# One-hots of the sort in 16 bits by sixteen instructions, their product on VectorE, and ctx splits behind the first gathers

## The reference

```python
x = x + xattn(layernorm(x), itok, ctx, ctx, ctx)     # Wg = Wu = Wd = ctx
x = x + ffn(layernorm(x), G, gate_w, up_w, down_w, lora_A, lora_B)

# xattn
tid = clip(token_ids, 0, 24999); expert_ids = minimum(tid // 6250, 3)
for e in range(4):
    y = (silu(h @ Wg[e].T) * (h @ Wu[e].T)) @ Wd[e].T
    out = where(expert_ids == e, y, out)

# ffn: scores = softmax(x @ G), top 2 of 8, w = their values in a row of 8
out = sum_e w[e] * ((silu(x @ gate_w[e].T) * (x @ up_w[e].T)) @ down_w[e].T + (x @ lora_A[e].T) @ lora_B[e].T)
```

## Time and profile before

| what | before |
|---|---|
| median of 3 runs | 313.19 us (311.81 to 313.78) |
| the profiled execution | 313.26 us |
| its span, first to last instruction | 311.5 us |
| PE busy | 266.6 us (86%) |
| DVE busy | 236.1 us (76%) |
| POOL busy | 168.6 us (54%) |
| ACT busy | 149.6 us (48%) |
| mean granted clock of TensorE | 0.925 |

### The profile page before, as it was taken

One profiled execution on the slowest core, in us unless ns is written; L12 is line 12 of the kernel. 1 busy time (PEld: TensorE's weight loads), 2 busy tenths in 40 slices (PEclk: granted clock), 3 DMA queues, 4 the chain that ended last, 5 costly groups with the idle time before them and its releaser, 6 DMA issues. The chain is left out here.

```text
span 311.5 us, 6118 instructions
## 1 busy us (share of the span) xinstructions
PE 266.6 (86%) x1629; PEld 230.0 (74%) x1629; DVE 236.1 (76%) x726; ACT 149.6 (48%) x350; POOL 168.6 (54%) x173
## 2 busy tenths in 40 slices
PE   0568999999999999999599949859999999999910
PEld 0546787888888887888488839748999899999700
DVE  8686848779987998799838985888999986666600
ACT  4532433444444445435324433226666678888810
POOL 3659425443488638863672181427544427867760
PEclk9958999999999999999789995679999999999965
DMA  7562999611043114410333035259977756999830
GB/s 272 198 207 76 337 241 333 233 34 38 0 157 103 36 34 170 162 43 2 136 137 102 2 136 170 80 149 313 303 245 208 216 176 92 208 247 151 106 51 0
DMA packets 23280, 45.98 MB, mean 148 GB/s; under 512 B 4540, under 2 KB 8636, under 8 KB 22656
## 3 DMA queue, kind: packets, MB, share of 16 engines
q0 software_dynamic: 9488, 21.84, 25.9%
q1 hardware_dynamic: 13760, 23.74, 25.2%
HBM read 24.49 MB, written 25.80 MB: 161 GB/s over the span
## 5 line engine op out<-in xcount | busy, mean ns | idle before, releaser
L399 POOL DMA_INDIRECT out<-pair_out,dest_now x38 | 49.8, 1311 | 32.5 <-DVE pair_out L924 13.4
L475 ACT ACTIVATE aT_hi<-p_aT 128x512 fp32r<-128x512 f32 x19 | 11.4, 600 | 55.3 <-PE p_aT L1038 55.3
L1112 PE MATMUL p_y<-ctx_hi,aT_hi 128*128 x76 | 32.6, 429 | 0.3 <-ACT aT_hi L475 0.3
L1112 PE MATMUL p_h<-ctx_hi,xT_hi 128*128 x72 | 29.9, 416 | 1.4 <-ACT xT_hi L471 1.4
L350 POOL DMA_INDIRECT xin<-x,gather_row x19 | 20.3, 1070 | 19.7 <-DVE rec L725 15.6
L1113 PE MATMUL p_y<-ctx_lo,aT_hi 128*128 x76 | 30.9, 406 | 0.0
L372 POOL DMA_INDIRECT rows_a<-rec,dest x19 | 18.9, 996 | 21.8 <-DVE dest L799 17.1
L1113 PE MATMUL p_h<-ctx_lo,xT_hi 128*128 x72 | 28.4, 395 | 0.0
L357 POOL TENSOR_TENSOR rstd<-var_eps,neg_half 128x1 f32<-128x1 f32 x19 | 12.7, 670 | 26.8 <-DVE var_eps L694 24.0
L1058 PEld LDWEIGHTS p_rt<-route_w,x2T 128*128 128x128 f32 x152 | 20.5, 198 | 3.9 <-issue 2.5
L486 ACT ACTIVATE rec<-rec,neg_mean 128x512 f32<-128x512 f32 x19 | 13.7, 723 | 18.3 <-DVE var_eps L734 17.4
(11 more groups left out here) (254 smaller groups left out, 792.7 us busy)
## 6 DMA issues: line engine op xcount, KB each, us to landing
whole<-ctx_t SPq DMA_DIRECT2D x4, 1024.0 KB, 6.7
pair_x_late<-rows_b SPq DMA_DIRECT2D x14, 258.0 KB, 4.3
pair_x_early<-rows_a SPq DMA_DIRECT2D x12, 258.0 KB, 3.2
pair_x_late<-rows_a SPq DMA_DIRECT2D x10, 258.0 KB, 3.7
whole<-w_up SPq DMA_DIRECT2D x4, 576.0 KB, 6.3
rows_a<-pair_x_early SPq DMA_DIRECT2D x8, 258.0 KB, 11.8
rows_b<-pair_x_early SPq DMA_DIRECT2D x8, 258.0 KB, 12.6
pair_x_early<-rows_b SPq DMA_DIRECT2D x8, 258.0 KB, 3.2
```

Of the source, the lines that this page charges most:

```text
L399: nc.gpsimd.indirect_dma_start(out=out, out_offset=bass.IndirectOffsetOnAxis(ap=rows, axis=0), in_=pair_out[:, s % ORING, :], in_offset=No ...
L1112: nc.tensor.matmul(to, hi(i), w_hi(i), start=(i == 0), stop=False)
```

## The change

Five edits.

- `col_h` is a 16 bit copy of `col` (0 to 127 in each partition), kept in the first columns of `x2T`, which isn't in use yet. `slot_lo` becomes a 32 bit float tensor copied from `slot_low`.
- The one-hots are sixteen tensor_scalar instructions of 128 numbers, with 16 bits in and out, and `slot_lo[:, c]` as a scalar for each partition. A semaphore is raised after every fourth, and TensorE waits for each group of four.
- The product `put[:, :, 0, :]` is made by DVE, ahead of the one-hots, and no longer by POOL.
- DVE's first split waits for `gathers_asked`, which a small POOL memset raises behind gathers 0 and 1. The DVE order becomes split (0,0), statistics(0), statistics(1) with normalise(0) inside, split (1,0), lo_x(0), normalise(1), split (1,1), split (2,0), statistics(2), split (2,1).
- `WARM` is 52 for 40.

```diff
-WARM = 40
+WARM = 52
+        col_h = x2T[:, 0:P // 2].bitcast(F16)
-        slot, slot_lo, slot_hi = (scrap(1980 + TILES * i, TILES).bitcast(I32) for i in range(3))
+        slot, slot_low, slot_hi = (scrap(1980 + TILES * i, TILES).bitcast(I32) for i in range(3))
+        slot_lo = scrap(2130, TILES)
+        gathers_asked = sem("gathers_asked")
...
-            pool.wait_ge(owners_ready, 1)
-            nc.gpsimd.tensor_tensor(put[:, :, 0, :], put[:, :, 1, :],
-                                    token_f.unsqueeze(2).broadcast_to([P, TILES, STEPS]),
-                                    ALU.mult).then_inc(puts_ready, 1)
             pool.wait_ge(rows_ready, 2)
             gather(0)
             gather(1)
+            nc.gpsimd.memset(x2T[:, D - 1:D], 0.0).then_inc(gathers_asked, 1)
             split_ctx(0, 1, ctx_lo_half_ready)
...
+            nc.vector.tensor_copy(col_h, col[:])
...
-            nc.vector.tensor_scalar(slot_lo, slot, P - 1, None, ALU.bitwise_and)
+            step(nc.vector.tensor_scalar(slot_low, slot, P - 1, None, ALU.bitwise_and))
+            nc.vector.tensor_copy(slot_lo, slot_low)
             step(nc.vector.tensor_scalar(slot_hi, slot, P.bit_length() - 1, None, ALU.logical_shift_right))
...
-            for half in range(2):
-                shape = [P, TILES // 2, P]
-                some = slice(half * TILES // 2, (half + 1) * TILES // 2)
-                nc.vector.tensor_tensor(in_lo[:, some, :], col[:].unsqueeze(1).broadcast_to(shape),
-                                        slot_lo[:, some].unsqueeze(2).broadcast_to(shape),
-                                        ALU.is_equal).then_inc(onehots_ready, 1)
+            dve.wait_ge(owners_ready, 1)
+            nc.vector.tensor_tensor(put[:, :, 0, :], put[:, :, 1, :], token_f.unsqueeze(2).broadcast_to(to_steps),
+                                    ALU.mult).then_inc(puts_ready, 1)
+            for c in range(TILES):
+                last = nc.vector.tensor_scalar(in_lo[:, c, :], col_h, slot_lo[:, c:c + 1], None, ALU.is_equal)
+                if c % 4 == 3:
+                    last.then_inc(onehots_ready, 1)
...
+            dve.wait_ge(gathers_asked, 1)
             split_ctx(0, 0)
-            split_ctx(1, 0)
             statistics(0)
             statistics(1, between=0)
-            split_ctx(1, 1)
+            split_ctx(1, 0)
             lo_x(0)
             normalise(1)
+            split_ctx(1, 1)
             split_ctx(2, 0)
...
-                if c % (TILES // 2) == 0:
-                    pe.wait_ge(onehots_ready, c // (TILES // 2) + 1)
+                if c % 4 == 0:
+                    pe.wait_ge(onehots_ready, c // 4 + 1)
```

## The result

The changed kernel takes 315.26 us in the median of 18 runs (314.38 to 316.7) against 313.06 for the kernel before in the same rounds (310.76 to 314.92): ratio 1.0077, 95% interval 1.0054 to 1.01, so it is 1.7 to 3.1 us slower. Forecast were 315.2 us and a difference of +2.0. The profiled execution took 315.98 us (span 314.2, before 311.5), somewhat over the median.

The account below looks back on a forecast made before the run. TensorE was taken to set the pace from 27.2 to 100 us, but at 34.16 to wait for the chain from statistics(2). That starts +1.4 and +0.6, so +2.0 us, later: 315.2 us on 313.19, range 312.3 to 317.0.

Parts of the forecast that it names:

- Where it decides: At 34.16 us, step 1's transposes of act wait for the DVE, POOL, DVE chain from statistics(2), without slack.
- Ahead of the one-hots: In the sort: waiting step, copy, shift and product on DVE start the first one-hot at 7.00 instead of 6.29, +0.71.
- The one-hots: In the sort: sixteen at 0.17 us each, 2.7 us in all; L658 starts +0.6 us later (-0.3 to +2.1).
- The first gather: With DVE idle until both gathers issue, it takes 1.0 us instead of 2.18; both done at 13.13, against 13.67.
- Rival 3: The first gather's 2.18 us is its own, not DVE's: +1.2 more, 316.4 us; chance 0.14.
- issues at 10.85, takes 1.0: The first gather issues at 10.85 instead of 10.21 and takes 1.0 us instead of 2.18.
- Who gets the port: Both first splits released at 13.13; POOL's goes first, DVE's stands until 15.55; normalise(0) at 18.45, +1.4 us.
- The order behind: Three splits between normalise(0) and statistics(2) instead of two: +1.13 less 0.51 idle, +0.6; statistics(2) at 24.2, +2.0.
- The sum: +2.0 us at step 1's transposes (36.2 for 34.16) carried to the end: 315.2 us on the median of 313.19.
- I see nothing later that gives it back: Behind the chain at 34.16 TensorE is full, so the +2.0 us stays to the end.
- rival 5: The lateness is taken up by a later load, or splits lie otherwise: within 0.5 us of before, 313; chance 0.08.
- The warm matmuls: Ahead of step 0: twelve more end near 14.7 us while TensorE is idle to 19.0, and cost nothing.

Follow-up runs that it names:

- run 1: The sort alone: one-hots, product and 52 warm matmuls as changed, splits as in the kernel before, no wait for gathers; 313.6 us, ratio 1.0033.
- run 2: The order alone: the kernel before with the new wait for gathers, the new split order and 52 warm matmuls; 314.06 us, ratio 1.0077.
- run 3: The changed kernel, but POOL's first split waits for DVE's split (0,0); 315.24 us, ratio 1.0064.
- run 5: The changed kernel plus one 128x1 POOL product when half the one-hots are made, before the first gather; 315.72 us, ratio 1.0088.
- run 4: The changed kernel with three sets of sixteen extra DVE instructions ahead of the one-hots, to price them; its one execution took 326.66 us.
- run 6: The changed kernel with 40 warm matmuls for 52; 315.46 us, ratio 1.0084.
- run 7: The kernel before with its start rebuilt (three gathers first, splits and constants moved), 40 or 84 warm matmuls; 313.1 and 313.03 us, ratios 1.0018 and 1.0014.
- run 8: The rebuilt start on the kernel before, constants moved to step 3, with 40, 84 or 104 warm matmuls; ratios 0.9976, 0.9974, 0.9994.

## Why the prediction was right, point by point

- **Where it decides.** Right: the chain from statistics(2) through POOL's splits to the transposes of step 1 carried the delay without slack (+2.88 at both ends; +0.32 and +0.31 in run 1, +1.03 and +1.01 in run 2, +1.59 and +1.57 in run 3, +2.27 and +2.24 in run 5).
- **Ahead of the one-hots.** +0.71 forecast, +0.98 measured (6.29 to 7.27). The term I left out is the copy of `col_h`: begun at 1.63 us it takes 0.81, while POOL's memsets run to 2.35, and the sort behind it comes 0.26 us later. The one-hots give 0.19 us back where 0.09 were forecast, so L658 of before starts 0.79 us late for +0.6.
- **The one-hots.** 0.17 us each forecast, 0.163 measured, and the terms behind it as well (run 4). Named once more, the rule of the Trainium skill (VectorE: DVE Perf Modes, the section on the TRN2 errata), 0.094 us: it comes near the immediate's 0.109 and leaves out the pointer's 0.054.
- **The first gather.** Rival 3 fell: alone it takes 1.16 us (run 2). The inference in the Trainium skill (SBUF — State Buffer, "Practical consequences"), that a two-input instruction doesn't hold up descriptor generation, does not fit: DVE's subtraction held this gather's issue for 1.0 us. The runs don't tell whether the writing of descriptors or the reading of `gather_row` out of SBUF was held. What failed is the step "issues at 10.85, takes 1.0": it issued at 11.65. 0.65 us of that is POOL's late start after a long idle time, which I hadn't priced; I had written the removal of POOL's product down as worth nothing, and it cost 0.65 (run 5). Another 0.15 is the sort (+0.79 at gather_row for +0.64) and 0.16 the gather itself (1.16 for 1.0). Gathers done at 14.10 for 13.13 forecast.
- **Who gets the port.** Right in kind and size: POOL first, the split at 3.36 us for "about 3.4"; run 3 takes just this away and normalise(0) comes 0.84 us earlier; the 1.31 us at step 1 hold some 0.4 of the clock.
- **The order behind.** +0.6 forecast from normalise(0) to statistics(2), +0.54 measured (25.08 - 19.37 against 22.20 - 17.03). Run 2, where it was +0.14 (23.23 - 17.92), shows that this term hangs on the clock: with the transposes at the upper clock DVE has no wait for lo_x(0).
- **The sum.** +2.0 forecast at step 1, +2.88 measured: 0.9 us too little, from 0.65 + 0.15 + 0.16 above. "I see nothing later that gives it back" was wrong by as much: 0.86 us is given back at step 3, as rival 5 had it in part. That the two cancel is luck, and so is the rest of the way in the trace, where the clock gives 0.9 and takes 1.4. The time, +2.2 us, so agrees better than its parts. What the times themselves bear out is that the order alone costs as much as the whole change by the ratio (1.0077 both) and the sort alone about 1 us; that the order costs it through the block stands on the traces.
- **The warm matmuls.** Nothing, as forecast (run 6).

Open: why the order alone is 1.3 us (medians) to 2.4 us (ratio) slower in time while its trace lags by 0.2 to 1.0; why neither the block taken away (run 3) nor the earlier gather (run 5) shows in the time; and whether the stretches at the lower clock, worth 0.9 and 1.4 us in these traces, follow from the kernel or change from one execution to the next.

## What to carry to other kernels

When a semaphore frees VectorE at the moment when GpSimd goes on to a long operation of two inputs in SBUF, expect that one of the two stands for the whole of the other's operation, and what is queued behind it too. The one that began 0.08 us earlier went first, POOL's split here and DVE's split against the first gather of the kernel before; but in the earlier trace rows POOL went first though its record begins 0.06 us later. A wait that fixes the order (run 3) is surer than a small difference in start. An operation taken off an engine can have been worth more than its result, and a cast "for later" that stands ahead of a serial chain is a term of the sum. A gain or loss of 2 us at a kernel's start is worth following to its end: a transfer whose landing did not move with the start took back 0.9 here.

## What the runs showed of the hardware

- GpSimd, idle for 9.3 us (changed kernel) or 16.5 (run 4), began an indirect DMA 0.95 us after its last input was written; having worked up to 2 us before, 0.30 (before, runs 2 and 5).
- An indirect DMA's issue of 1.16 us took 2.18 beside a two-input subtraction on VectorE that had begun 0.08 us earlier (before and run 2).
- Sixteen tensor_scalar of 128 numbers on VectorE: 0.109 us each with an immediate, 0.163 with a pointer scalar (16 bits), 0.204 from 32 bit integers.
- A small operation was held as the large ones were: 0.17 us became 4.36 behind two GpSimd subtractions in a row, and it wasn't let in between them (run 7).
- TensorE's clock stayed at its upper level for 2.3 us after the warm matmuls of the kernel before (13.0 to 15.3), and for some 5 us after those of the changed kernel (14.3 to 19.4). With 84 warm matmuls begun at 9.5 us it fell at 19.2 in run 7 and at 25.2 in run 8.
